# Edge pass of a graph layer: the dense branch in double pieces over the first seventeen half groups

## The reference, cut to what matters

```python
q, k, v = (x @ Wq + bq), (x @ Wk + bk), (x @ Wv + bv)      # 4 heads of 64
alpha = sum(q[dst] * k[src], axis=-1) / 8
a = exp(alpha - segment_max(alpha, dst)[dst])
out = segment_sum(a * v[src], dst) / segment_sum(a, dst) + (x @ Ws + bs)
...
x1 = x + xf                                    # x1 is linear in x once the 64x64 attention is known
h = gelu(layernorm(x1) @ w_fc1 + b_fc1) @ w_fc2 + b_fc2    # 256 -> 768 -> 256
mix = x1 + h
...
x = x + out + mix
x = x + experts(layernorm(x))
```

## Time and profile before

| | us |
|---|---|
| median of 3 runs | 2742.48 (2741.88 to 2743.84) |
| the profiled execution's own time | 2726.39 |
| its span, first to last instruction | 2724.7 |
| edge pass in the trace, first one hots to last sums | about 431.9 to 1812.7 |

### The profile page before, as it was taken

How to read it: one execution, slowest core, us unless ns; L and a number is a source line. 1 busy time by engine, 2 the same in 40 slices (tenths; PEclk the granted TensorE clock), 3 DMA queues, 4 the chain that set the end, 5 groups by cost and what they waited for, 6 DMA issues and landing times.

```text
span 2724.7 us, 40541 instructions
## 1 busy us (share of the span) xinstructions
PE 2420.6 (89%) x13040; PEld 2027.1 (74%) x13040; DVE 2041.9 (75%) x3437; ACT 1346.3 (49%) x2549; POOL 962.9 (35%) x890
## 2 busy tenths in 40 slices
PE   6378995698989989998899899858999999999998
PEld 4257774577777777777777777648888888888898
DVE  6797453698888888888889888856666666666665
ACT  5421110265556566556565565655555555455553
POOL 0240004576677677676767676400000000000000
PEclk9689997899999999999999999979999999999999
DMA  5130456576676676676676676520000000000000
GB/s 153 34 118 31 141 174 200 171 218 197 194 216 203 201 217 203 194 219 195 206 212 206 194 214 190 159 88 9 15 16 16 16 16 17 16 16 14 14 9 12
DMA packets 186670, 336.17 MB, mean 123 GB/s; under 512 B 28104, under 2 KB 125680, under 8 KB 186438
## 3 DMA queue, kind: packets, MB, share of 16 engines
q0 software_dynamic: 67104, 219.09, 26.8%
q1 hardware_dynamic: 119366, 114.51, 13.8%
HBM read 293.82 MB, written 40.48 MB: 123 GB/s over the span
## 4 chain that ended last, share of the span: by engine, by line
PE 57%; DVE 17%; ACT 10%; another core or an unknown queue 7%; issue 7%; DVEq 1%; ACTq 1%; DMA 0%; POOL 0%; SPq 0%; POOLq 0%
PE ps L1438 20%; PE ps L1448 10%; PE ps L1336 8%; PE ps L1191 5%; PE ps L1325 3%; DVE ring L1792 3%; ACT nodes L968 3%; ACT keys L948 2%; DVE ring L1847 2%; DVE rows L1535 2%; PE ps L1104 2%; PE ps L1270 1%; PE ps L1111 1%; DVE nodes L1861 1%
## 5 line engine op out<-in xcount | busy, mean ns | idle before, releaser
L839 POOL DMA_INDIRECT ring<-kv_rows,idx x832 | 910.9, 1095 | 650.0 <-DMA kv_rows<-work 247.8
L1438 PE MATMUL ps<-f_split,e_up 128*128 128x512 f32 (+1 forms) x1664 | 502.3, 383 | 7.2 <-DVE e_low L2005 6.8
L1325 PE MATMUL ps<-nodes,ohT 128*128 x1664 | 416.5, 395 | 68.6 <-issue 49.2
L1336 PE MATMUL ps<-ring,keys 128*128 128x260 f32 x1664 | 436.2, 407 | 0.1
L1325 PEld LDWEIGHTS ps<-nodes,ohT 128*128 128x128 f32 x1664 | 318.7, 196 | 140.9 <-issue 97.7
L1029 ACT ACTIVATE f_more<-ps,e_rest 128x512 f32<-128x512 f32 (+1 forms) x416 | 289.1, 745 | 268.7 <-PE ps L1438 267.9
L1981 DVE TENSOR_TENSOR f_split<-f_more,f_split 128x1024 fp32r<-128x1024 f32 (+1 forms) x208 | 242.0, 1164 | 237.4 <-ACT f_split L1035 233.8
L1438 PEld LDWEIGHTS ps<-f_split,e_up 128*128 128x128 f32 x1664 | 306.1, 190 | 55.1 <-DVE e_low L2005 7.5
L1336 PEld LDWEIGHTS ps<-ring,keys 128*128 128x128 f32 x1664 | 311.9, 197 | 41.6
L1438 PE MATMUL ps<-f_split,e_low 128*128 128x512 f32 (+1 forms) x832 | 315.6, 379 | 0.0
L1792 DVE TENSOR_TENSOR ring<-ring,ps 128x1024 f32<-128x1024 f32 x208 | 252.2, 1212 | 73.4 <-remote 42.2
(11 more groups left out here) (347 smaller groups left out, 3271.1 us busy)
## 6 DMA issues: line engine op xcount, KB each, us to landing
relq<-rel_rows SPq DMA_DIRECT2D x208, 128.0 KB
ring<-kv_rows,idx POOLq DMA_INDIRECT x832
kv_rows<-work SPq DMA_DIRECT2D x49, 256.0 KB, 2.2
xn_rows<-nodes SPq DMA_DIRECT2D x1, 6272.0 KB, 22.3
sx_rows<-work SPq DMA_DIRECT2D x49, 128.0 KB, 1.7
nodes<-in_x_dram SPq DMA_DIRECT2D x4, 1536.0 KB
work<-in_x_dram SPq DMA_DIRECT2D x48, 128.0 KB, 2.3
m_xn<-xn_rows SPq DMA_DIRECT2D x24, 256.0 KB
```

The costliest lines, as they stand in the source:

```text
L839: pool.indirect_dma_start(out=kvh(i)[:, g, 0:2 * D], out_offset=None, in_=kvD, in_offset=bass.IndirectOffsetOnAxis(ap=idx[c // KP][:, s:s ...
L1325: last = pe.matmul(ps[:, 2048 + D * g:2048 + D * (g + 1)], ohT[c % 2][:, g * P:(g + 1) * P], nodes[:, ds(win[g] * AC + HG * AC, D)], start ...
L1336: last = pe.matmul(to, keys[j % 2][:, g * P:(g + 1) * P], kvh(j)[:, g, D:SL], start=(g == 0), stop=False, skip_group_check=True)
L1438: last = pe.matmul(bank(2 * l + m, 0, n * P), e_parts[l][w][:, e, i, m * P:(m + 1) * P], src_[a][:, i * QW:i * QW + n * P], start=(i == 0 ...
```

## The change

`dense` goes, and `pieces(i)` takes its place. With `FAST` = 17 and `HEAD` = 6, step i < 17 does the two pieces 6 + 2i and 7 + 2i, and a later step the one piece i + 23. That is 24 pieces, three groups, further on than before, and the piece's place in its group, (i - 1) % 8, is the same as before in every step from 17 on. The pieces 2 to 5 of group 0 are run ahead of step 0: on PE between the first turning of rows and `spread_q(1)`, on ACT behind the first copy, on DVE between `row_one_hots(0)` and step 0. On every engine both pieces of a step stand at the place where the one stood; on PE both `mix` come ahead of both `mix_behind`. The last piece of the dense branch is at step 184 on SP, and at step 183 on the others. SP's separate store of the last group behind the loop goes.

```diff
-    def dense(c, m):
-        return m * (U // PIECES) + (c - SHIFT) // PIECES, (c - SHIFT) % PIECES
+    def pieces(i):
+        at = range(HEAD + 2 * i, HEAD + 2 * i + 2) if i < FAST else (i + FAST + HEAD,)
+        return [(q // PIECES, q % PIECES) for q in at]
...
-                g, p = dense(c, m)
+                for g, p in pieces(i):
+                    mix_moves(g, p)
...
-            if (NG + 1) * PIECES + SHIFT + 7 >= NHF:
-                mix_store(NG, tiles_of(NG))
...
             act.wait_ge(sem("acc_zero"), 1)
             mix_turned(0, TG)
+            for p in range(2, HEAD):
+                mix(0, p)
...
-                g, p = dense(c, m)
-                mix(g, p)
+                for g, p in pieces(i):
+                    mix(g, p)
...
-                mix_behind(g, p)
+                for g, p in pieces(i):
+                    mix_behind(g, p)
...
             mix_turn(0, TG)
+            for p in range(2, HEAD):
+                mix(0, p)
+                mix_behind(0, p)
             spread_q(1, 1, windows_of(1))
...
             row_one_hots(0, 0, 0)
+            for p in range(2, HEAD):
+                mix(0, p)
```

More of the change, by code:

```diff
@@ L78, in gps_layer_kernel @@
     WL = H * (CS + 1)
-    SHIFT = 1
+    FAST = 17
+    HEAD = 6
     U = 2 * KP
-    TURNS = NHF // U
     LAST = NHF + LAG + 1
     assert NW % 7 == 0 and NW == NG * TG + 1 and NE == 8 and NHF % CH == 0 and KP % CH == 0 and U % PIECES == 0
-    assert TURNS * U // PIECES == NG and (NG + 1) * PIECES + SHIFT + 6 < NHF and CS * H <= P
+    assert (NG + 1) * PIECES + 7 - FAST - HEAD < NHF and (FAST + HEAD + 1) % PIECES == 0 and CS * H <= P
     HI = HT // (2 * G)
@@ L604, in step, with mix_moves @@
                     idx_load(m * 2 + (b + 1), 1 - b)
-                g, p = dense(c, m)
+                for g, p in pieces(i):
+                    mix_moves(g, p)
+            def mix_moves(g, p):
                 if p == 0 and g >= 2 and tiles_of(g - 1):
```

## The result

The change makes the kernel slower. Medians of 12 runs each are 2734.57 us before and 2758.28 us after (2745.33 to 2767.17); the ratio is 1.0083, with a 95% interval of 1.0061 to 1.0105, so some 23 us. The profiled execution after took 2745.33 us beside 2726.39 before. It is the fastest of its twelve, so the traces differ by 19 us, and the 5 us between that and the medians lie in no trace. In the code after, gathers are L841, the spread of q L1329, sums L1340, first layer L1274, gelu L944, score products L1800, scores L1806.

A forecast was written before the change was run, and what follows sets the result against it. In the long middle PE (91% busy) and DVE (87%) were taken as the bound together, POOL close behind. +11 - 18 - 3 = -10 us, from 2742.5 to 2732.5 us; range 2719 to 2753, the forecast's own 2726 to 2737.

The forecast's parts named there:

- (a): Pass start up to the fifth products: the head's delay of 3 us is covered by the stop ending at 482.74 us; 0.
- the alternative I named: Up to the fifth products: if the stop there follows the head, +5 us instead of 0.
- (b): From the fifth products to step 17: 26 pieces where 13 stood, 23.6 + 7.4 - 11 - 5 - 4 = +11 us.
- my terms (+7.4 - 11 - 4): Fifth products to step 17: waits within steps +7.4 us, idle time filled -11, waits on the 509.08 us stop -4.
- that of the first-layer pieces: Fifth products to step 17: second first-layer piece waits for two gelus and two signals, 1.1 us in four steps.
- (c): Last 24 steps with scores lose their dense pieces, POOL's pace becomes the bound: -18 us (-9.6 to -26).
- PE's 33.5 us: Last steps with scores: PE work lost, 14.9 + 13.7 us in two large instruction groups, 4.9 in small ones.
- (d): Behind the pass: SP's dense store leaves the drain and W1's load comes some 30 us earlier; -3 us (0 to -4).
- the dear front: Rival, chance 0.18: in-step waits make the front cost more than the end gives, (b) +28, about 2754 us.
- the missing gain: Rival, chance 0.17: waits in the last steps stay, a chain over PE, DVE and ACT; about 2742 us.
- The clock rival: Rival, chance 0.05: PE's clock falls at the end without dense work; a third at lower level costs 30 us, 2762.
- my sign: Steps behind 184: a clock below 0.9 there would show the forecast wrong.

The follow-up runs named there:

- e6: The changed kernel as it is, on a chip where PE's signals came on time; ratio 1.0100 to the kernel before on the same chip.
- e5: The kernel before as it is, profiled on a chip with signals on time, where it took about 2575 us.
- e9: The kernel before with three of four gathers from half group 184 on, part of the edge sums not computed, on the late-signal chip; ratio 0.9912.
- e7: The changed kernel with FAST = 1, one dense group moved instead of three, signals on time; ratio 1.0020 to the kernel before.
- e8: The changed kernel with FAST = 9, two dense groups moved instead of three, signals on time; ratio 1.0038 to the kernel before.
- e12: The changed kernel with the second piece of a double step behind spread_q on PE, on the late-signal chip; ratio 1.0133 to the kernel before.

## Why the prediction was wrong

The sum was +11 - 18 - 3; the trace has +21.7, then -1.9 in the long middle, then -0.8 at the end, and -1.5 behind products 207.

- *(a), 0.* It was +5.1, the alternative I named: the stop follows the head. It moved from products 4 to products 2 (23.3 us from products 1 to 2), and products 4 are late by what the head's pieces and that stop make together.
- *(b), +11.* It was +14.0 by products 17 and +16.6 by products 24, since step 16's pair delays products 18 (11.1 us). From products 4 to 24 PE's busy time grew from 101.7 to 121.0 us, as 23.6 less 5 for the clock had it. Its idle time fell only from 18.4 to 15.7, where my terms (+7.4 - 11 - 4) make -7.6. The term that failed is that of the first-layer pieces: 4.4 us, against 12.1 us of waits at L1274 (1.9 before). I priced such a wait as one gelu and two signals and left out what ACT does ahead of the gelu, the table load, and late signals. Another 14.2 us of such waits lie ahead of products 4, in (a). Of the 26.3 us in all, e6 has 8.3, so most of them came with the late signals.
- *(c), -18.* It was -4.3 in the steps 176 to 184, where I had 4, and +3.5 instead of -14 in the 23 steps behind. I had POOL's own price right (132 us for 23 steps; 130.3 in e6), but took it as reachable from 144.1. On the chip of record the stretch is at nobody's pace, before or after: by the comparisons with e5, e9 and e6 late signals make up some 19 us of the one and 17 of the other. Freed of dense work PE and DVE keep up with POOL in the short steps (4.3 us at products 191 and 199), POOL's runs there grow from at most 24 gathers to 28, three times, and the stops give it all back. PE's 33.5 us were also too many, its busy time fell by 23.0: busy times of groups overlap (all of them in the earlier trace rows's stretch add up to 142.6 us, of 128.6), and without its dense instructions the trace before is busy for 101.5 us there, where the one after has 105.5, at a mean granted clock of 0.86 instead of 0.94. For the same reason the 14.5 us a group are too many: the first two groups add 11.4 and 11.3 us to PE's busy time in the front (e7, e8). Without late signals the sum would have been wrong too: there PE and POOL bound the stretch at nearly the same pace (125.4 and 130.3 us, the first with some of POOL's lead used up), and nothing came back.
- *(d), -3.* -1.5. No edit of its own tells what part of this is the store or the load; where signals are on time the drain grew by 4.9 us (e6).

So two steps of the working failed: (c), which took POOL's pace as a price that the stretch of record could fall to, and (a) with (b), which priced the waits of the doubled pieces without late signals and took the first stop as fixed.

The rivals: what came is the dear front and the missing gain at once, which I had given 0.18 and 0.17 as separate cases. Neither needs the late signals: without them the front is dearer still (31.2 us at products 24 in e6, 39.1 us more of PE's work against 7.9 us less of its idle time), and nothing comes back at the end. What the late signals changed is how both came about on the chip of record, and there I passed over that the wait of the earlier trace rows was a signal under way and not an engine at work. The rule of the Trainium skill on shared ports (SBUF — State Buffer, Who interferes with whom), by which (c) would be -25, moved little: gathers in the last stretch took 1096 ns instead of 1116. The clock rival came in part: the last stretch's mean fell from 0.94 to 0.86, below the 0.9 of my sign, but for some 4 us of PE's busy time and not 30. In the drain of the runs of record it didn't fall (0.89 before, 0.93 after, from products 207 to the last weighing).

## What to carry to other kernels

Before work is moved out of a stretch, ask of each engine whether it ever waits there: where POOL's idle time was almost all "issue" (e5, e6), nothing taken from PE or DVE shortened the stretch. Idle time at this pass's start took one portion of extra work for nothing (one group, 0.2 us), and even that cost 0.2% in the whole, at the other end. Two dependent pieces in one step wait for each other's chain, with all that the other engine has queued ahead of its part. A long wait for an engine that by the trace has already finished may be a late signal; look what runs without a pause beside it, and whether the change lengthens those runs, as it did here from 24 gathers to 28.

## What the hardware showed that was not expected

PE's signals, and PE's alone, came up to 15 us late in the runs of record (up to 19.6 in e12) and on one of the four chips of the experiments. How they go with POOL's gathers, in the trace before, up to products 207:

- Of the 25 signals over 4 us late 22 came in a pause of POOL, 18 of them 1.4 to 2.8 us behind the run's last gather. (After: 20 of 27, and 15.)
- Of the 151 that were 1 to 4 us late 87 came while a run went on.
- The matmul that sent a late signal ended within a run in 97% of the cases; that of a signal on time in 82%. POOL is in a run most of the time, so this alone would prove little; the weight is on e9.

On the three other chips the same program with the same gathers (1098 ns each in e5) ran up to 824 of them without a pause and had no late signal, and it was 6 to 7% faster: 5.66 us a step instead of 6.3 to 6.5. So runs of gathers are not enough by themselves. What differs between the chips stays open.
